# Compressed interaction network on one core: a smaller copy of layer 0's weights, another order of the first loads, and layer 2's weights read during the first two periods

## The chip, the cores and the metric

The kernel runs on one core of one Trainium2 chip. The metric is device time in microseconds (us) of one execution, as the median of several; lower is better. Engines are named as in the profile: PE multiplies matrices, DVE works element by element, ACT evaluates functions and copies, POOL does a little setup, and SP issues the transfers, which sixteen DMA engines carry out.

## The reference

For 512 rows of 39 fields of 32 numbers, three layers each form all products of a field with a hidden row, multiply them by a weight matrix and apply a ReLU:

```python
hidden = x                                        # [512, 39, 32]
for i in range(3):
    z = jnp.einsum('bmd,bnd->bmnd', x, hidden).reshape(B, -1, D)
    cur = jax.nn.relu(jnp.einsum('bcd,co->bod', z, Ws[i]) + bs[i][None, :, None])   # 200 rows out
    if i != 2: hidden, direct = cur[:, :100], cur[:, 100:]
    else:      direct = cur
    finals.append(direct)
return jnp.sum(jnp.concatenate(finals, axis=1), axis=-1)                            # [512, 400]
```

W0 is [39 x 39, 200]; W1 and W2 are [39 x 100, 200]; all is float32.

## The kernel before

The 512 x 32 pairs of row and position are cut into 128 units of 128 columns. For a unit, DVE forms products (L361 for layer 0, L380 for layers 1 and 2, L367 for four chunks of layer 2 that are multiplied whole), ACT rounds them to a high part (L525), DVE subtracts to get a low part (L384), and PE multiplies both by the weights, which are held in a high and a low part side by side in the `w_split` tiles (L659, L660; L647 for the whole chunks). Products live in a ring of three buffers. PE transposes the hidden half (L671), ACT spreads it (L541 to L544), and so the next layer's products can be made.

The order of the work is written out by hand, for each engine apart, and semaphores tie the engines together. In the steady state a period n handles layer 1 of unit n, layer 0 of unit n + 2 and layer 2 of unit n - 1. Period 0, ahead of the function `period`, has layer 1 of unit 0 and layer 0 of unit 2 alone; period 1 is the first with layer 2. A loop runs four periods at a time.

Ahead of period 0 stands the prologue, which the change rewrites:

- Layer 0 needs each unordered pair of fields once, so it needs the sum of two reads of W0: one along columns, one along rows, both starting at the diagonal and wrapping around after field 38. To let a plain strided read wrap, SP first copies W0 in DRAM to two tensors that hold it one and a half to two times over: `w0_columns_again` (L227, L228) and `w0_rows_again` (L229, L230). After both copies have landed, six loads (L241, L244) bring the strided rows into `pair_w` and `pair_w2`, 39 SBUF rows for each of three shifts; a seventh (L247) brings the bias. DVE adds the two (L413), ACT and DVE split the sum (L553, L416). The two buffers lie inside tile `xb0`.
- x is turned in DRAM into `x_by_unit`, one batch of units at a time (`turn_x`, L185 and L186), from where `load_pairs` (L191, L192) and `load_xb` (L198 to L204) fetch each unit's operands.
- W1 and W2 come in four groups each (`load_w`, L213, L215, L221, L223) through two staging halves inside tile `xb1`, numbered k = 0 to 7. For each group ACT writes the high part (L553), DVE the low part (L349). The last group of a layer has seven extra loads of four rows each (L221), after DVE has zeroed their rows (L345).
- PE's first multiplication of layer 1 waits until all eight groups are split, W2's too (L687).

SP issues every transfer, in one queue; an issue that waits for a semaphore holds all that stand behind it.

Of the kernel before, what the change touches and what calls it, by code (L numbers as in the profile page):

```python
# [5 lines left out]
F32 = mybir.dt.float32  # L6
# [4 lines left out]
P = 128  # L11
# [17 lines left out]
XROWS = F + SHIFTS * L0_CHUNKS - 1  # L29

# [47 lines left out]
def cin_kernel(nc, r_x, W0, W1, W2, b0, b1, b2, out):  # L78
    x, w0 = r_x.tensor, W0.tensor
    xt = nc.dram_tensor("x_by_unit", [UNITS, XROWS, T], F32)  # L80
    w0c = nc.dram_tensor("w0_columns_again", [F, 2 * F, O], F32)
    w0r = nc.dram_tensor("w0_rows_again", [2 * F, F, O], F32)
    xt_t, w0c_t, w0r_t = xt.ap().tensor, w0c.ap().tensor, w0r.ap().tensor

    with ExitStack() as ctx:
# [19 lines left out]
        z = [sb(f"z{i}", [P, GROUP * T]) for i in range(RING)]  # L105
# [10 lines left out]
        o_row = {l: sb(f"o_row{l}", [BT, DIRECT[l]]) for l in range(3)}  # L116
# [42 lines left out]
        stage_all = xb[1][:, :, :].rearrange("p c t -> p (c t)")  # L159

        def stage(k):
            at, n = (k % 2) * GROUP * O, group_chunks(k % GROUPS)
            return stage_all[:, at:at + n * O].rearrange("p (c o) -> p c o", o=O)
# [5 lines left out]
        pair_w = xb[0][:, :, :].rearrange("p c t -> p (c t)")[:, 0:L0_CHUNKS * O].rearrange("p (c o) -> p c o", o=O)  # L169
        Q = L0_CHUNKS * O  # L170
        pair_w2 = xb[0][:, :, :].rearrange("p c t -> p (c t)")[:, Q:2 * Q].rearrange("p (c o) -> p c o", o=O)

# [5 lines left out]
        def _(sp):  # L178
# [29 lines left out]
            def load_w(k, w, bias):  # L208
                g = k % GROUPS
                a, n = GROUP * g, group_chunks(g)  # L210
                wt, row = w.tensor, HID * O
                st = stage(k)
                sp.dma_start(st[0:MAIN, :, :], bass.AP(wt, a * row, [[O, MAIN], [row, n], [1, O]])).then_inc(w_in[k], 16)  # L213
                if g < GROUPS - 1:
                    sp.dma_start(st[MAIN:P, :, :],  # L215
                                 bass.AP(wt, CHUNKS * row + 32 * g * O, [[O, P - MAIN], [row, n], [1, O]])).then_inc(w_in[k], 16)
                else:
                    for j in range(TAIL_M):
                        n = min(TAIL_CHUNKS, F - TAIL_CHUNKS * j)
                        at = MAIN + TAIL * j  # L220
                        sp.dma_start(st[at:at + TAIL, 0:n, :],  # L221
                                     bass.AP(wt, TAIL_CHUNKS * j * row + MAIN * O, [[O, TAIL], [row, n], [1, O]])).then_inc(w_in[k], 16)
                    sp.dma_start(st[ONES_ROW:ONES_ROW + 1, 0, :], bass.AP(bias.tensor, 0, [[O, 1], [1, O]])).then_inc(w_in[k], 16)  # L223

            turn_x(0, 0)
            n2 = XROWS - F
            sp.dma_start(bass.AP(w0c_t, 0, [[2 * F * O, F], [1, F * O]]), bass.AP(w0, 0, [[F * O, F], [1, F * O]])).then_inc(w0_again[0], 16)  # L227
            sp.dma_start(bass.AP(w0c_t, F * O, [[2 * F * O, F], [1, n2 * O]]), bass.AP(w0, 0, [[F * O, F], [1, n2 * O]])).then_inc(w0_again[0], 16)  # L228
            sp.dma_start(bass.AP(w0r_t, 0, [[F * O, F], [1, F * O]]), bass.AP(w0, 0, [[F * O, F], [1, F * O]])).then_inc(w0_again[1], 16)  # L229
            sp.dma_start(bass.AP(w0r_t, F * F * O, [[F * O, n2], [1, F * O]]), bass.AP(w0, 0, [[F * O, n2], [1, F * O]])).then_inc(w0_again[1], 16)  # L230
# [3 lines left out]
            turn_x(0, 1)  # L234
            sp.wait_ge(cleared, 2)
            sp.wait_ge(w0_again[0], 32)
            sp.wait_ge(w0_again[1], 32)
            for k in range(SHIFTS):
                last = len(range(k, L0_PAIRS, SHIFTS))
                at = slice(k * F, (k + 1) * F)  # L240
                sp.dma_start(pair_w[at, 0:last, :],  # L241
                             bass.AP(w0c_t, k * O, [[(2 * F + 1) * O, F], [SHIFTS * O, last], [1, O]])).then_inc(pairs_w_in, 16)
                c = 1 if k == 0 else 0
                sp.dma_start(pair_w2[at, c:last, :],  # L244
                             bass.AP(w0r_t, (k + SHIFTS * c) * F * O, [[(F + 1) * O, F], [SHIFTS * F * O, last - c], [1, O]]))\
                  .then_inc(pairs_w_in, 16)
            sp.dma_start(pair_w[L0_ONES:L0_ROWS, 0, :], bass.AP(b0.tensor, 0, [[O, 1], [1, O]])).then_inc(pairs_w_in, 16)  # L247
            load_w(0, W1, b1)
            load_w(1, W1, b1)
# [4 lines left out]
            for k in range(2, 2 * GROUPS):  # L254
                sp.wait_ge(w_low_done, k)
                if k % GROUPS == GROUPS - 1:
                    sp.wait_ge(stage_ready, k // GROUPS + 1)
                load_w(k, W1 if k < GROUPS else W2, b1 if k < GROUPS else b2)
                if k == GROUPS - 1:
                    sp.wait_ge(ones_set, 1)  # L260
                    for g in range(GROUPS):
                        load_xb(0, 0, g)
            sp.wait_ge(xt_done, 96)
            turn_x(0, 3)
            sp.wait_ge(xt_done, 128)
            turn_x(1, 0)
            sp.wait_ge(product, 2)
            load_pairs(2)
            sp.wait_ge(ones_set, 2)
            for g in range(GROUPS):  # L270
                sp.wait_ge(xb_in[g], XB_COUNT[g])
                load_xb(1, 1, g)

            def send(l, rows):
                sp.wait_ge(o_in[l], rows + 1)
                sp.dma_start(bass.AP(out.tensor, rows * (BT * OUT_COLS) + OUT_AT[l], [[OUT_COLS, BT], [1, DIRECT[l]]]), o_row[l][:, :])\
                  .then_inc(o_out[l], 16)
# [65 lines left out]
        def _(dve):  # L343
            def stage_zeros(k):
                return nc.vector.memset(stage(k)[MAIN:P, :, :], 0.0)  # L345

            def low_w(k, dst, st):
                dve.wait_ge(w_high_done, k + 1)
                nc.vector.tensor_tensor(dst[:, :, O:2 * O], st, dst[:, :, 0:O].bitcast(F32), ALU.subtract).then_inc(w_low_done, 1)  # L349
# [6 lines left out]
            def product0(u, number, slot):  # L356
                slot_read(number)
                dve.wait_ge(pairs_in, 96 * (u + 1))
                left = x_left[0:L0_ROWS, :].unsqueeze(1).to_broadcast([L0_ROWS, L0_CHUNKS, T])
                dst = z[slot][0:L0_ROWS, 0:L0_CHUNKS * T].rearrange("p (c t) -> p c t", t=T)  # L360
                nc.vector.tensor_tensor(dst, left, x_right[0:L0_ROWS, :, :], ALU.mult).then_inc(product, 1)  # L361
# [7 lines left out]
            def product12(layer, u, par, g, number, slot):  # L369
# [9 lines left out]
                dst = z[slot][:, 0:n * T].rearrange("p (c t) -> p c t", t=T)  # L379
                nc.vector.tensor_tensor(dst, left, xb[par][:, c0:c0 + n, :], ALU.mult).then_inc(product, 1)  # L380

            def lows(number, slot, rows, n):
                dve.wait_ge(high, number + 1)
                nc.vector.tensor_tensor(z_low[slot][0:rows, 0:n * T], z[slot][0:rows, 0:n * T],  # L384
# [9 lines left out]
            def directs(l, rows, q):  # L394
# [8 lines left out]
                else:  # L403
                    dve.wait_ge(direct_in[l], u)
                    nc.vector.scalar_tensor_tensor(direct[l][:, :], part, 0.0, direct[l][:, :], ALU.max, ALU.add).then_inc(direct_in[l], 1)  # L405

            nc.vector.memset(x_left[MAIN:P, :], 1.0).then_inc(ones_l0, 1)
            nc.vector.memset(x_right[MAIN:P, :, :], 1.0).then_inc(ones_l0, 1)
            nc.vector.memset(pair_w, 0.0).then_inc(cleared, 1)
            nc.vector.memset(pair_w2, 0.0).then_inc(cleared, 1)  # L410
# [4 lines left out]
            dve.wait_ge(w_high_done, 1)  # L415
            nc.vector.tensor_tensor(w_split[0][0:L0_ROWS, :, O:2 * O], pair_w[0:L0_ROWS, :, :],  # L416
                                    w_split[0][0:L0_ROWS, :, 0:O].bitcast(F32), ALU.subtract).then_inc(w_low_done, 1)
            product0(0, 0, 0)
            lows(0, 0, L0_ROWS, L0_CHUNKS)
            for k in range(2 * GROUPS):  # L420
                l, g = 1 + k // GROUPS, k % GROUPS
                low_w(1 + k, piece(l, g), stage(k)[:, split_from(l, g):, :])
                if k in (1, 5):
                    dve.wait_ge(w_low_done, k + 2)
                    stage_zeros(k + 2).then_inc(stage_ready, 1)
                if k == 1:
                    dve.wait_ge(w_low_done, 1)
                    nc.vector.memset(xb[0][MAIN:P, TAIL_AT:CHUNKS, :], 1.0).then_inc(ones_set, 1)
                    product0(1, 1, 1)
                    lows(1, 1, L0_ROWS, L0_CHUNKS)  # L430
                    sums(0, 0)
                if k == 2:
                    directs(0, 0, 0)
                if k == 3:
                    sums(0, 1)
            dve.wait_ge(w_low_done, 1 + 2 * GROUPS)
            nc.vector.memset(xb[1][MAIN:P, TAIL_AT:CHUNKS, :], 1.0).then_inc(ones_set, 1)


            directs(0, 0, 1)  # L440
# [7 lines left out]
            lows(at + 4, slot_of(at + 4), L0_ROWS, L0_CHUNKS)  # L448
            sums(1, 0)
            sums(0, 2)  # L450
            directs(1, 0, 0)
            directs(0, 0, 2)

            def period(m, j, base, sl, layer0=True, before0=True, before2=True, last_low=True):
# [5 lines left out]

                product12(1, n, par, 0, base, slot(0))
                if last_low:
                    lows(base - 1, slot(-1), P, group_chunks(3))
# [57 lines left out]
        def _(act):  # L521
# [36 lines left out]
            for k in range(2 * GROUPS):  # L558
# [13 lines left out]
                if k == 5:  # L572
                    dup(0, 1)
# [198 lines left out]
```

## Time and profile before

| | |
|---|---|
| median of 3 runs | 2790.6 us (2790.5 to 2791.17) |
| the profiled execution's own time | 2791.72 us |
| its span, first to last instruction | 2790.0 us |
| PE busy | 2702.3 us, 97% |
| DVE busy | 2667.3 us, 96% |
| ACT busy | 1698.4 us, 61% |
| DMA, mean | 120 GB/s |

The span is what lies between the first and the last instruction; the execution has 1.7 us around it. In the profile's forty slices (69.75 us each) PE is over 90% busy in all but the first two: the prologue lies in these. A busy PE need not be at its peak, so what a wait costs is read from when the next stage starts.

### The profile page before, as it was taken

To read this page: it belongs to the slowest core of one execution; us is meant where nothing else is said; L and a number is where in the kernel's file an instruction comes from. 1 tells how busy PE (TensorE), PEld (TensorE's weight loads), DVE (VectorE), ACT (ScalarE), POOL (GpSimd) and SP (SyncE) were. 2 spreads that over 40 slices of the span, in tenths; PEclk is the share of its full clock that TensorE was granted. 3 is DMA by queue.
4 is the path that set the end of the run, shared out by engine and by line. 5 is a ranking of instruction groups with operands and counts; after the bars stand their busy time and mean duration, and the time that the engine had idled before them with its cause. 6 is when DMAs were issued, how large, how long until landed. Compare 5 with 4: busy or idle time off the path is not lost.

```text
span 2790.0 us, 56206 instructions
## 1 busy us (share of the span) xinstructions
PE 2702.3 (97%) x18112; PEld 2661.2 (95%) x18112; DVE 2667.3 (96%) x3218; ACT 1698.4 (61%) x3179; POOL 1.2 (0%) x11
## 2 busy tenths in 40 slices
PE   1799999999999999999999999999999999999999
PEld 1799999999999999999999999999999999999998
DVE  3799999999999999999999999999999999999997
ACT  2566666666666666666666666666666666666664
POOL 0000000000000000000000000000000000000000
PEclk9999999999999999999999999999999999999999
DMA  8454544454554454454454454445444445444541
GB/s 194 109 128 110 129 122 108 120 133 108 125 128 109 114 139 109 115 131 115 108 136 117 109 128 124 108 125 128 108 121 122 118 116 132 112 111 123 127 108 59
DMA packets 346786, 333.97 MB, mean 120 GB/s; under 512 B 151970, under 2 KB 281614, under 8 KB 346638
## 3 DMA queue, kind: packets, MB, share of 16 engines
q1 hardware_dynamic: 346762, 333.67, 48.0%
q8 instruction: 13, 0.21, 0.0%
q14 instruction: 11, 0.09, 0.0%
HBM read 332.73 MB, written 8.37 MB: 122 GB/s over the span
## 4 chain that ended last, share of the span: by engine, by line
PE 82%; DVE 8%; issue 4%; DMA 3%; ACT 2%; SPq 1%; DVEq 0%; ACTq 0%
PE acc L659 51%; PE acc L660 24%; PE acc L647 5%; DVE z_low L384 4%; DVE z L380 2%; DMA xb<-x_by_unit 1%; PE summed L677 1%; PE turned L671 1%; ACT z_high L525 1%; DMA xb<-in_L_rec_b_dram 1%; DVE z L361 1%; ACT hid L544 0%; DMA w_rows_again<-in_L_rec_W_dram 0%; DMA xb<-in_L_rec_W_dram 0%; DVE w_split L349 0%
## 5 line engine op out<-in xcount | busy, mean ns | idle before, releaser
L659 PE MATMUL acc<-w_split,z_high 128*128 128x400 f32 (+1 forms) x8320 | 2511.8, 369 | 64.6 <-DVE z_low L384 58.5
L660 PE MATMUL acc<-w_split,z_low 128*128 128x200 f32 (+1 forms) x8320 | 2120.5, 255 | 0.0
L525 ACT ACTIVATE z_high<-z 128x1024 fp32r<-128x1024 f32 (+3 forms) x1152 | 1125.0, 977 | 882.4 <-DVE z L380 728.3
L659 PEld LDWEIGHTS acc<-w_split,z_high 128*128 128x128 f32 (+1 forms) x8320 | 1565.4, 188 | 88.5 <-issue 78.4
L660 PEld LDWEIGHTS acc<-w_split,z_low 128*128 128x128 f32 (+1 forms) x8320 | 1593.0, 191 | 0.0
L384 DVE TENSOR_TENSOR z_low<-z,z_high 128x1024 fp32r<-128x1024 f32 (+3 forms) x1152 | 1282.5, 1113 | 45.3 <-ACT z_high L525 45.0
L380 DVE TENSOR_TENSOR z<-hid,xb 128x1024 f32<-128x1024 f32 (+2 forms) x1024 | 1142.0, 1115 | 11.2 <-DMA xb<-x_by_unit 10.9
L544 ACT ACTIVATE hid<-turned 32x128 f32<-32x128 f32 x768 | 205.3, 267 | 8.9
L541 ACT ACTIVATE hid<-turned 96x512 f32<-96x512 f32 x256 | 150.4, 588 | 91.8 <-PE turned L671 91.6
L647 PE MATMUL acc<-w_whole,z_whole 128*128 128x200 f32 x1024 | 197.7, 336 | 3.1 <-DVE s L391 3.1
L647 PEld LDWEIGHTS acc<-w_whole,z_whole 128*128 128x128 f32 x1024 | 168.9, 190 | 3.4 <-DVE s L391 3.4
L391 DVE TENSOR_TENSOR s<-acc,half 128x200 f32<-128x200 f32 x384 | 137.1, 357 | 8.9 <-ACT half L530 8.9
L361 DVE TENSOR_TENSOR z<-x_left,x_right 118x896 f32<-118x896 f32 x128 | 138.4, 1081 | 0.0
L530 ACT ACTIVATE half<-acc 128x200 f32<-128x200 f32 x384 | 126.9, 331 | 16.4 <-PE acc L660 10.9
L367 DVE TENSOR_TENSOR z_whole<-hid,xb 128x512 f32<-128x512 f32 x128 | 87.5, 684 | 5.8 <-ACT hid L544 5.8
L671 PE MATMUL turned<-ident,s 128*128 128x128 f32 x256 | 69.9, 273 | 16.5 <-ACT s L535 16.5
L405 DVE SCALAR_TENSOR_TENSOR direct<-s,direct 128x100 f32<-128x100 f32 (+1 forms) x288 | 83.0, 288 | 0.1
L542 ACT ACTIVATE hid<-turned 32x128 f32<-32x128 f32 x256 | 69.3, 271 | 3.0
L535 ACT ACTIVATE s<-s 128x24 f32<-128x24 f32 x256 | 52.4, 205 | 1.3 <-DVE s L391 1.3
L671 PEld LDWEIGHTS turned<-ident,s 128*128 128x128 f32 x256 | 36.0, 141 | 17.1 <-ACT s L535 17.1
L550 ACT ACTIVATE o_row<-summed 16x100 f32<-16x100 f32 (+1 forms) x96 | 25.5, 266 | 37.2 <-PE summed L677 36.4
L677 PE MATMUL summed<-direct,group_b 128*16 128x100 f32 (+1 forms) x192 | 38.5, 282 | 1.2 <-DVE direct L405 1.2
(25 smaller groups left out, 72.0 us busy)
## 6 DMA issues: line engine op xcount, KB each, us to landing
xb<-x_by_unit SPq DMA_DIRECT2D x384, 384.0 KB, 4.4
x_right<-x_by_unit SPq DMA_DIRECT2D x384, 136.5 KB
xb<-x_by_unit SPq DMA_DIRECT2D x384, 128.0 KB, 5.0
xb<-x_by_unit SPq DMA_DIRECT2D x128, 336.0 KB
xb<-x_by_unit SPq DMA_DIRECT2D x128, 84.0 KB
x_left<-x_by_unit SPq DMA_DIRECT2D x384, 19.5 KB
xb<-in_L_rec_W_dram SPq DMA_DIRECT2D x6, 600.0 KB, 9.4
x_by_unit<-in_r_x_dram SPq DMA_DIRECT2D x128, 19.5 KB
```

The lines of the kernel that those rows point to most:

```text
L361: nc.vector.tensor_tensor(dst, left, x_right[0:L0_ROWS, :, :], ALU.mult).then_inc(product, 1)
L380: nc.vector.tensor_tensor(dst, left, xb[par][:, c0:c0 + n, :], ALU.mult).then_inc(product, 1)
L384: nc.vector.tensor_tensor(z_low[slot][0:rows, 0:n * T], z[slot][0:rows, 0:n * T], z_high[slot][0:rows, 0:n * T].bitcast(F32), ALU.subtract ...
L391: nc.vector.tensor_tensor(s[l][:, :, 0:HID], acc[l][:, 0:O].rearrange("p (h o) -> p h o", o=HID), half[l][:, :, :], ALU.add)\
L525: nc.scalar.activation(z_high[slot][0:rows, 0:n * T], z[slot][0:rows, 0:n * T], ACT.Copy).then_inc(high, 1)
L530: nc.scalar.activation(half[l][:, :, :], acc[l][:, O:2 * O].rearrange("p (h o) -> p h o", o=HID), ACT.Copy)\
L541: nc.scalar.activation(h[0:MAIN, :, :], turned[l][0:MAIN, 0:T].unsqueeze(1).to_broadcast([MAIN, GROUPS, T]), ACT.Relu)
L544: last = nc.scalar.activation(h[MAIN:P, g, :], turned[l][32 * g:32 * (g + 1), 0:T], ACT.Relu)
L647: last = nc.tensor.matmul(acc[2][:, 0:O], z_whole[par][:, c * T:(c + 1) * T], w_whole[:, c, :], start=(c == 0), stop=False, skip_group_che ...
L659: nc.tensor.matmul(a[:, 0:2 * O], z_high[slot][0:rows, tok], w, start=(c == 0), stop=False, skip_group_check=True)
L660: last = nc.tensor.matmul(a[:, 0:O], z_low[slot][0:rows, tok], w[:, 0:O], start=False, stop=(c == chunks - 1), skip_group_check=True)
L671: nc.tensor.transpose(turned[l][:, 0:T], s[l][:, 0, :], ident[:, :]).then_inc(turned_in[l], 1)
```

## The change

Four things move.

1. The copies in DRAM hold only what must wrap. `NEAR` is 20, `REST` is 19. For fields 0 to 19 the six strided loads read W0 itself. For fields 20 to 38 they read two small copies, written by four copies of 19 rows of 3800 numbers. So layer 0's weights come in twelve loads and a bias instead of six and a bias, and DVE waits for 13 where it waited for 7.
2. Buffers: `pair_w` and `pair_w2` lie in the ring of products, now one tile `z`; groups 0 and 1 of W1, and all groups of W2, are staged in a tile `stage2` of their own, and only groups 2 and 3 of W1 in `xb1`. The rows for the outputs lie in `stage2` too.
3. SP's order: W0's first parts, the pairs of unit 0, W0's rest, then W1's groups, each followed by the part of `xb` that period 0 multiplies with it, then W2's first two groups, and W2's last two behind the `xb` of unit 1.
4. W2's groups are split on ACT and DVE in period 0 (the first) and period 1 (the other three), and PE waits for W1 alone ahead of period 0, for W2 ahead of period 1's layer 2. The layer-1 sums of unit 0 and layer-0 sums of unit 2 move from the gap between the two periods into period 1.

The core of the diff (the waits and the reordering of ACT and PE are of the same kind as DVE's):

```diff
+NEAR = L0_PAIRS
+REST = F - NEAR
...
-    w0c = nc.dram_tensor("w0_columns_again", [F, 2 * F, O], F32)
-    w0r = nc.dram_tensor("w0_rows_again", [2 * F, F, O], F32)
+    w0c = nc.dram_tensor("w0_columns_again", [REST, 2 * REST, O], F32)
+    w0r = nc.dram_tensor("w0_rows_again", [2 * REST, REST, O], F32)
...
+            def load_w0(near):
+                f0, n = (0, NEAR) if near else (NEAR, REST)
+                cols, rows = (w0, w0) if near else (w0c_t, w0r_t)
+                per_col, per_row = (F, F) if near else (2 * REST, REST)
+                for k in range(SHIFTS):
+                    last = len(range(k, L0_PAIRS, SHIFTS))
+                    at = slice(k * F + f0, k * F + f0 + n)
+                    sp.dma_start(pair_w[at, 0:last, :],
+                                 bass.AP(cols, k * O, [[(per_col + 1) * O, n], [SHIFTS * O, last], [1, O]])).then_inc(pairs_w_in, 16)
...
-            sp.dma_start(bass.AP(w0c_t, 0, [[2 * F * O, F], [1, F * O]]), bass.AP(w0, 0, [[F * O, F], [1, F * O]])).then_inc(w0_again[0], 16)
...
+            for half, (col, row) in enumerate([(NEAR, NEAR), (0, 0)]):
+                sp.dma_start(bass.AP(w0c_t, half * REST * O, [[2 * REST * O, REST], [1, REST * O]]),
+                             bass.AP(w0, w0_rest + col * O, [[F * O, REST], [1, REST * O]])).then_inc(w0_again[0], 16)
+                sp.dma_start(bass.AP(w0r_t, half * REST * REST * O, [[REST * O, REST], [1, REST * O]]),
+                             bass.AP(w0, row * F * O + NEAR * O, [[F * O, REST], [1, REST * O]])).then_inc(w0_again[1], 16)
+            sp.wait_ge(cleared, 2)
+            load_w0(True)
+            sp.dma_start(pair_w[L0_ONES:L0_ROWS, 0, :], bass.AP(b0.tensor, 0, [[O, 1], [1, O]])).then_inc(pairs_w_in, 16)
             sp.wait_ge(xt_done, 32)
             sp.wait_ge(ones_l0, 2)
             load_pairs(0)
-            turn_x(0, 1)
...
+            load_w0(False)
+            turn_x(0, 1)
+            sp.wait_ge(ones_set, 1)
+            for g in range(2):
+                load_w(sp, 1, g, W1, b1)
+                load_xb(0, 0, g)
...
-            dve.wait_ge(pairs_w_in, 16 * 7)
+            dve.wait_ge(pairs_w_in, 16 * 13)
...
-            pe.wait_ge(w_low_done, 1 + 2 * GROUPS)
-            pe.wait_ge(w_whole_in, 1)
+            pe.wait_ge(w_low_done, 1 + GROUPS)
...
+                else:
+                    pe.wait_ge(w_low_done, 1 + 2 * GROUPS)
+                    pe.wait_ge(w_whole_in, 1)
                 multiply_whole(n - 1, 1 - j % 2)
```

What stands on SP's queue near its start, before the change: the four copies and then the first loads of unit 0's pairs. The last column is rows by columns of the destination.

```order
L227 DMA w_columns_again<-in_L_rec_W_dram 39x7800
L228 DMA w_columns_again<-in_L_rec_W_dram 39x4000
L229 DMA w_rows_again<-in_L_rec_W_dram 30x10140
L230 DMA w_rows_again<-in_L_rec_W_dram 16x9750
L191 DMA x_left<-x_by_unit 39x128
L192 DMA x_right<-x_by_unit 39x7x128
```

The same place of the changed program: four copies of 19 rows, then the first of six loads that read W0 itself.

```order
L247 DMA w_columns_again<-in_L_rec_W_dram 19x3800
L249 DMA w_rows_again<-in_L_rec_W_dram 19x3800
L247 DMA w_columns_again<-in_L_rec_W_dram 19x3800
L249 DMA w_rows_again<-in_L_rec_W_dram 19x3800
L237 DMA z<-in_L_rec_W_dram 20x7x200
L240 DMA z<-in_L_rec_W_dram 20x6x200
```

Each copy has 19 rows of 15.2 KB where the first one had 39 of 31.2 KB. Further down SP's queue in the changed program, behind the pairs of unit 0, stand the six loads from the copies, then the second batch of x and W1's first group.

```order
L214 DMA x_right<-x_by_unit 39x7x128
L237 DMA z<-w_columns_again 19x7x200
L240 DMA z<-w_rows_again 19x6x200
L237 DMA z<-w_columns_again 19x7x200
L240 DMA z<-w_rows_again 19x7x200
L237 DMA z<-w_columns_again 19x6x200
L240 DMA z<-w_rows_again 19x6x200
L207 DMA x_by_unit<-in_r_x_dram 624x1x8
L208 DMA x_by_unit<-in_r_x_dram 320x1x8
L182 DMA stage<-in_L_rec_W_dram 96x8x200
```

These six loads had 39 rows each before; all W1 loads stand behind them. On DVE, in period 1, the changed program has this between its second and its third product of layer 1:

```order
L403 TENSOR_TENSOR z<-hid_1,xb 128x1024
L407 TENSOR_TENSOR z_low<-z,z_high 128x1024
L414 TENSOR_TENSOR s<-acc,half 128x2x100
L425 TENSOR_SCALAR direct<-s 128x100
L363 TENSOR_TENSOR w_split<-stage,w_split 128x8x200
L369 MEMSET stage 32x1400
L403 TENSOR_TENSOR z<-hid_1,xb 128x1024
L407 TENSOR_TENSOR z_low<-z,z_high 128x1024
L428 SCALAR_TENSOR_TENSOR direct<-s,direct 128x100
L363 TENSOR_TENSOR w_split<-stage,w_split 128x8x200
L403 TENSOR_TENSOR z<-hid_1,xb 128x896
```

Before, the products and low parts of that place followed each other directly; now sums, two low parts of W2 (L363) and a memset stand among them.

## Rows read from the trace of the kernel before

**Rows 1.** Chain that ended last, first 140 us: start, length in us, what.

```profile
5.26 11.92 DMA w_rows_again<-in_L_rec_W_dram
20.25 7.89 DMA xb<-in_L_rec_b_dram
...
76.06 1.38 ACT w_split L553
77.46 1.62 DVE w_split L349
...
115.54 1.37 PE acc L647 x8
```

**Rows 2.** Timeline: start, us, engine, line, operation, count, idle before and its releaser.

```profile
28.16 1.62 DVE L413 TENSOR_TENSOR xb<-xb 118x1400 f32<-118x1400 f32 x1 [23.11 <-DMA xb<-in_L_rec_b_dram]
62.05 0.87 ACT L562 ACTIVATE w_whole<-xb 128x800 f32<-128x800 f32 x1 [8.70 <-DMA xb<-in_L_rec_W_dram]
80.34 2.35 DVE L380 TENSOR_TENSOR z<-hid,xb 128x1024 f32<-128x1024 f32 x2
```

**Rows 3.** PE's waits from 140 us to 2780 us: total, times, longest.

```profile
PE acc L647 <- DVE s L391: 3.1, 1, 3.1
```

**Rows 4.** Windows, 157 to 240 us: busy us of PE, PEld, DVE, ACT, POOL.

```profile
157.00:240.00 83.00, 83.00 (x561) 81.84 (x561) 81.58 (x100) 51.69 (x99) 0.00 (x0) 1.00 0.48 117
```

**Rows 5.** DMA packets that start from 4.0 to 5.4 us, in 40 slices.

```profile
GB/s 21 13 14 3 0 0 0 0 0 891 3566 1783 891 1783 1783 891 0 0 0 0 0 0 0 0 0 0 0 0 0 0 0 0 0 0 0 0 0 0 0 0
DMA packets 75, 0.41 MB, mean 291 GB/s; under 512 B 62, under 2 KB 62, under 8 KB 62
```

**Rows 6.** Windows; the last two columns are DMA share of sixteen engines and GB/s.

```profile
6.00:10.00 4.00, 0.00 (x0) 0.00 (x0) 0.00 (x0) 0.00 (x0) 0.00 (x0) 1.00 0.86 314
7.00:7.50 0.50, 0.00 (x0) 0.00 (x0) 0.00 (x0) 0.00 (x0) 0.00 (x0) 1.00 1.50 624
...
20.00:22.00 2.00, 0.00 (x0) 0.00 (x0) 0.00 (x0) 0.00 (x0) 0.00 (x0) 1.00 0.90 147
42.00:60.00 18.00, 4.36 (x15) 3.99 (x15) 6.81 (x8) 6.09 (x11) 0.00 (x0) 1.00 1.06 223
72.00:72.50 0.50, 0.00 (x0) 0.00 (x0) 0.19 (x1) 0.28 (x1) 0.00 (x0) 1.00 1.14 381
73.50:74.50 1.00, 0.00 (x0) 0.00 (x0) 0.64 (x1) 0.00 (x0) 0.00 (x0) 1.00 0.27 69
```

**Rows 7.** SP's issues in the timeline: start, us taken to issue.

```profile
8.83 4.86 SPq L185 DMA_DIRECT2D x_by_unit<-in_r_x_dram  x1
...
70.04 2.50 SPq L221 DMA_DIRECT2D xb<-in_L_rec_W_dram  x7
```

**Rows 8.** DMA issues of the whole run: KB each, median us to landing.

```profile
out_dram<-o_row SPq DMA_DIRECT2D x64, 6.2 KB, 1.4
```

**Rows 9.** Window of PE's first eight chunks of layer 1, columns as in rows 4.

```profile
84.00:88.50 4.50, 4.39 (x16) 4.39 (x17) 4.50 (x5) 1.06 (x1) 0.00 (x0) 1.00 0.86 240
```

**Rows 10.** Timeline: the splitting of W2, the hidden rows of layer 0, two sums.

```profile
63.71 0.99 DVE L349 TENSOR_TENSOR w_split<-xb,w_split 128x800 fp32r<-128x800 f32 x1 [9.96 <-ACT w_split L553]
64.64 1.54 ACT L553 ACTIVATE w_split<-xb 128x1600 fp32r<-128x1600 f32 x1 [0.96 <-DMA xb<-in_L_rec_W_dram]
...
66.21 1.82 DVE L349 TENSOR_TENSOR w_split<-xb,w_split 128x1600 fp32r<-128x1600 f32 x1 [1.51 <-ACT w_split L553]
...
68.39 1.23 DVE L345 MEMSET xb<- 32x1400 f32 x1 [0.35 <-DVE w_split L349]
...
77.34 0.57 ACT L541 ACTIVATE hid<-turned 96x512 f32<-96x512 f32 x1
...
78.21 0.82 ACT L544 ACTIVATE hid<-turned 32x128 f32<-32x128 f32 x3
...
96.09 0.37 DVE L391 TENSOR_TENSOR s<-acc,half 128x200 f32<-128x200 f32 x1 [2.70 <-ACT half L530]
98.14 0.37 DVE L391 TENSOR_TENSOR s<-acc,half 128x200 f32<-128x200 f32 x1 [1.69 <-ACT half L530]
```

More of the change, by code:

```diff
@@ L206, in load_xb @@
                       .then_inc(xb_in[g], 16)
[L208 to L223, printed above, removed]
@@ L253, in _ @@
             load_pairs(1)
[L254 to L262, printed above, removed]
+            for g in range(2, GROUPS):
+                load_w(sp, 1, g, W1, b1)
+                load_xb(0, 0, g)
             sp.wait_ge(xt_done, 96)
             turn_x(0, 3)
+            for g in range(2):
+                sp.wait_ge(w_low_done, g + 2)
+                load_w(sp, 2, g, W2, b2)
+            sp.wait_ge(product, 2)
+            load_pairs(2)
             sp.wait_ge(xt_done, 128)
             turn_x(1, 0)
-            sp.wait_ge(product, 2)
-            load_pairs(2)
+            sp.wait_ge(w_low_done, 5)
             sp.wait_ge(ones_set, 2)
@@ L418, in _ @@
+            dve.wait_ge(w_low_done, 1)
             product0(0, 0, 0)
             lows(0, 0, L0_ROWS, L0_CHUNKS)
[L420 to L435, printed above, removed]
@@ L436, in _ @@
-            dve.wait_ge(w_low_done, 1 + 2 * GROUPS)
-            nc.vector.memset(xb[1][MAIN:P, TAIL_AT:CHUNKS, :], 1.0).then_inc(ones_set, 1)
+            low_piece(1, 1, 0)
+            sums(0, 0)
+            low_piece(2, 1, 1)
+            product0(1, 1, 1)
+            lows(1, 1, L0_ROWS, L0_CHUNKS)
+            directs(0, 0, 0)
+            low_piece(3, 1, 2)
+            sums(0, 1)
+            low_piece(4, 1, 3)
+            dve.wait_ge(w_low_done, 5)
+            ones(1)
             directs(0, 0, 1)
@@ L447, in _, with period @@
             lows(at + 3, slot_of(at + 3), P, group_chunks(3))
[L448 to L454, printed above, removed]
+            low_piece(5, 2, 0)
+            def period(m, j, base, sl, layer0=True, before0=True, before2=True):
                 n, par = m * QUARTERS + j, j % 2
@@ L459, in slot @@
                     return (sl + p) % RING
+                second = not before2
                 product12(1, n, par, 0, base, slot(0))
-                if last_low:
+                if second:
+                    lows(base - 1, slot(-1), L0_ROWS, L0_CHUNKS)
+                    sums(1, 0)
+                else:
                     lows(base - 1, slot(-1), P, group_chunks(3))
-                if before0 and last_low:
-                    directs(0, m + (j + 1) // QUARTERS, (j + 1) % QUARTERS)
+                    if before0:
+                        directs(0, m + (j + 1) // QUARTERS, (j + 1) % QUARTERS)
                 product12(1, n, par, 1, base + 1, slot(1))
                 lows(base, slot(0), P, group_chunks(0))
+                if second:
+                    sums(0, 2)
+                    directs(1, 0, 0)
+                    low_piece(6, 2, 1)
+                    dve.wait_ge(w_low_done, 7)
+                    stage_zeros(2)
                 product12(1, n, par, 2, base + 2, slot(2))
                 lows(base + 1, slot(1), P, group_chunks(1))
+                if second:
+                    directs(0, 0, 2)
+                    low_piece(7, 2, 2)
                 product12(1, n, par, 3, base + 3, slot(3))
@@ L495, in period @@
                     sums(0, n + 2)
-            period(0, 1, first(1), first(1) % RING, before2=False, last_low=False)
+            period(0, 1, first(1), first(1) % RING, before2=False)
             period(0, 2, first(2), first(2) % RING)
@@ L524, in highs @@
                 act.wait_ge(product, number + 1)
-                nc.scalar.activation(z_high[slot][0:rows, 0:n * T], z[slot][0:rows, 0:n * T], ACT.Copy).then_inc(high, 1)
+                nc.scalar.activation(z_high[slot][0:rows, 0:n * T], z[0:rows, slot, 0:n * T], ACT.Copy).then_inc(high, 1)
             def second_half(l, u, last):
@@ L590, in slot @@
                     return (sl + p) % RING
+                second = not before2
                 highs(base, slot(0), P, group_chunks(0))
-                if before0:
+                if second:
+                    second_half(1, 0, base - 2)
+                elif before0:
                     dup(0, n + 1)
                 highs(base + 1, slot(1), P, group_chunks(1))
-                hidden(1, n - 1, 1 - par)
+                if second:
+                    second_half(0, 2, base - 1)
+                    dup(1, 0)
+                    high_piece(2, 1)
+                    dup(0, 2)
+                else:
+                    hidden(1, n - 1, 1 - par)
                 highs(base + 2, slot(2), P, group_chunks(2))
+                if second:
+                    hidden(1, 0, 0)
+                    high_piece(2, 2)
                 if before2:
@@ L608, in period @@
                     q = 5
+                if second:
+                    high_piece(2, 3)
                 if j == 2:
@@ L702, in period @@
                 acc_free(1, n)
+                second = not before2
                 multiply(1, base, slot(0), 0)
-                if before0:
+                if before0 and not second:
                     transpose(0, n + 1)
@@ L708, in period @@
                 multiply(1, base + 1, slot(1), 1)
+                if second:
+                    transpose(1, 0)
+                    transpose(0, 2)
                 if j == 2:
```

145 lines of the change are left out of this document (78 added, 67 removed).

## The prediction

> **What bounds the kernel now.** I read the chain of waits of the first 140 us, then the timeline of that stretch, then the waits of the rest. From about 140 us on PE is the pace: it waits 3.1 us for one operation and little else up to 2780 us [rows 3]; between 157 and 240 us PE is busy 83.00 of 83 us and DVE 81.58 [rows 4], so DVE has only some 1.4 us of room in four periods. The prologue is another matter. PE's first multiplication of whole chunks, the mark where layer 2 of unit 0 begins, is at 115.54 us [rows 1]; from there the two programs do the same work, some 2674 us of it. So the change is worth what it moves this mark.
>
> I cut the time up to the mark in three. First, W0: DVE can add the two reads of W0 at 28.16 us, after waiting 23.11 us for a DMA [rows 2]; behind it stand the copy (11.92 us at 5.26) and the loads (7.89 us at 20.25) [rows 1]. Second, from there to the first product of layer 1 at 80.34 us [rows 2], 52.2 us, in which W1 and W2 arrive through two halves of one buffer; ACT alone waits 8.70 us for W2's first group [rows 2]. Third, from that product to the mark, 35.2 us.
>
> **Part 1, W0: how many DMA engines a transfer of 19 rows uses.** The first copy has 39 rows of 31.2 KB. Of the packets that start between 4.0 and 5.4 us 75 - 62 = 13 are over 8 KB, 0.41 MB or 13 x 31.2 KB; they start within 0.3 us, and then none starts for 0.8 us, though 26 rows of this copy, and more copies, are queued [rows 5]. So 13 engines work, three rows each, not sixteen. Near 74 us the seven loads of four rows of W2's last group drain: DMA share 0.27, which is 4.3 of sixteen engines, at 69 GB/s [rows 6]; they were issued within 2.5 us [rows 7], so had each taken other engines, all sixteen would have been at work. What fits both rows: the rows are dealt in equal shares, 13 x 3 and 4 x 1, always to the same first engines. A transfer of 19 rows then has equal shares only on one engine, since no number from 2 to 16 divides 19; one of 20 rows has ten.
>
> The Trainium skill ("DMA: Bandwidth & Descriptors", section "Why a DMA increments its semaphore by 16 and not by 1") states this as a rule: the transfer runs on the largest k up to 16 that divides the slowest dimension of both sides, and on this queue on the lowest-numbered k engines. By that rule the changed copies and the loads from them have k = 1; the trace agrees at 39 and 4 rows, and no run here shows 19. The Trainium skill's same page (section "Specifications") gives about 27 GiB/s per engine, by which the four copies would take an estimated 40 us.
>
> The terms, then:
> - Copies: 4 x 19 x 15,200 B = 1.155 MB through one engine. A busy engine moves GB/s over 16 x share: 624/(16 x 1.50) = 26.0 GB/s at best and 314/(16 x 0.86) = 22.8 over four us of the copies [rows 6]. I take 26.0, as nothing else disturbs one engine: 44.4 us (at 22.8: 50.7). From 4.0 us: 48.4. Before, the four copies (3.6 MB) took from 4 to 17.2 us [rows 1], three times the bytes in a third of the time.
> - Behind them on the same engine lie its shares of the loads from W0 itself (78 rows of 800 B) and of unit 0's pairs (72 rows of 512 B), 99 KB at 16 GB/s: 6.2 us. They cover SP's wait for the copies.
> - The six loads from the copies: 19 x 39 = 741 rows of 800 B, 0.593 MB. For rows of this size an engine moved 69/(16 x 0.27) = 16.0 GB/s where four worked, 381/(16 x 1.14) = 20.9 at best, 147/(16 x 0.90) = 10.2 where 13 read these same layouts [rows 6]. I take 16.0, the row with the fewest engines: 37.1 us (28.4 to 58.1).
> - Landing: 1.4 us, as for a small output [rows 8].
>
> W0 is complete at 48.4 + 6.2 + 37.1 + 1.4 = 93.1 us instead of 28.2: **+64.9 us**. Nothing hides it: W1's loads stand behind on the same queue, and everything on DVE, ACT and PE starts from W0. The loads behind may run ahead on the fifteen idle engines, but SP was held 4.86 us in one issue when about 130 rows per engine lay queued [rows 7], and one engine's share of all that follows is still to come; I take nothing for it, and up to 6 us as its bound.
>
> **Part 2, from W0 to the first product of layer 1.** W2 no longer stands here. What must land is W1 (3066 KiB), three parts of `xb` (1536), the pairs of unit 1 (468) and two batches of x (60): 5.25 MB, at the 223 GB/s of the long full stretch [rows 6] 23.6 us, plus 1.4 to land [rows 8]. Then the last group is split, a memset and one sum follow: 76.06 to 80.34 before, 4.3 us [rows 1, 2]. Together 29.3 instead of 52.2: **-22.9 us**. The work on ACT and DVE in between (each W1 group about 1.5 and 1.8 us) is shorter than the loads and hidden by them. Bounds: 24 us if loads run ahead, 35 if the 223 GB/s is too high by a fifth.
>
> **Part 3, the first product to the mark.** W2's split now lies here. DVE has four low parts, 0.99 + 1.82 + 1.82 + 1.62, and the memset, 1.23: 7.5 us [rows 1, 10], on an engine without room. Each low part waits for ACT's high part, and ACT's own queue decides: for the first group twice 0.87 us, whole and split half [rows 2]; for the second 1.54, less a short sum; for the last about 1.4 after ACT's products. The third is worst: ACT does it after the hidden rows of unit 0, these wait for PE's transposes, those for eight chunks on PE (4.39 us at half clock [rows 9], near half that at full), and these eight wait for a low part that DVE now makes only after the second group and its memset. From that low part: 2.2 to 4.4 for PE, two transposes, 1.7 for the hidden rows (0.57, then four short ones, three of which take 0.82) and 1.54 for ACT's high part [rows 10], 6 to 8 us in which DVE has nothing else. I add 1.9 + 1.3 + 7 + 1.9 = 12 us of waits. Taken away: DVE's 2.70 and 1.69 us ahead of the sums between the periods [rows 10], since a product now comes first. 35.2 + 7.5 + 12 - 4.4 = 50.3: **+15.1 us**. Bounds: 43 (waits covered) to 55.
>
> W2's loads of 0.8 MB each land far ahead of this, except the last, issued when the second group is split: 2.50 us for its small issues [rows 7] and 3 us of data at 223 GB/s, within the third group's wait.
>
> **Sum.** 64.9 - 22.9 + 15.1 = +57.1 us at the mark. After it DVE leads PE by about 2 us less; with its 1.4 us of room per four periods that could show as up to 2 us more, which I leave in the range. On the profiled execution's 2791.7 us (span 2790.0 and 1.7 around it) this is 2848.8; the median of the runs is 1.1 lower, so **2847 us**.
>
> **Rivals.**
> - *Rows dealt over many engines.* If 19 rows went to 16 engines unevenly, the change does what its parts promise: copies 1.155 MB at 314 GB/s [rows 6], 3.7 us; SP issues nineteen more transfers up to about 15 us, and W0 lands near 20. Then 20 + 29.3 + 50.3 = 99.6, 15.9 before the old mark: 2775 us, faster. It decides the sign, from the point where copies and loads together take under about 30 us. Against it: 39 rows went to 13, where an uneven deal would have used 16.
> - *One engine per transfer, but another each time.* Copies side by side, 289 KB at 26 GB/s, 11.1 us; each load 133 rows, 6.7 us; W0 near 25 us: 2780. Against it: the seven loads of four rows stayed on 4.3 engines.
> - *One engine, and the loads at 10.2 GB/s*, the rate at which these layouts were read: 58.1 instead of 37.1 us, 2868. For it: the same strides; against it: then 13 engines and the turning of x shared the memory.
>
> **How the numbers follow.** The forecast has 0.80; its own range is 2829 (loads at 20.9 GB/s and 6 us of running ahead, 8.7 + 6 less, and part 3 at its low end) to 2864 (copies at 22.8, +6.3, part 2 and 3 at their high ends). The slow loads have 0.10, the many engines 0.06, other engines 0.03; 0.01 is left for a mixture near no change. A difference of 0.2%, 5.6 us, is what a measurement of this kernel can tell from none. Slower by more: 0.90; faster: 0.09; same: 0.01. The range takes in the slow loads: 2829 to 2868.
>
> **What would show it.** In the trace after: between about 5 and 45 us packets over 8 KB start one at a time, near 0.6 us apart, with a DMA share near 0.06 of sixteen; SP stands in the issues of the loads; DVE waits for W0 until some 93 us (81 to 115); the first product of layer 1 comes about 29 us later, the mark about 50 after that; in period 1 DVE waits 6 to 8 us for ACT ahead of W2's third group, and PE starves with it. Four or more large packets starting together in the copies, or W0 complete ahead of 35 us, would prove the first step wrong, and the sign with it.

## The result, and the profile after

The changed kernel takes 2834.9 us (median of four runs, 2833.5 to 2835.5) where the kernel before takes 2790.65: a ratio of 1.0158, with a 95% interval of 1.014 to 1.0175. It is slower by 44.3 us; forecast was 2847, slower by 56.

The profiled execution took 2835.5 us. Part 1 of its page, the span and the busy time of the engines:

```profile
span 2833.8 us, 56212 instructions
PE 2705.9 (95%) x18112; PEld 2664.7 (94%) x18112; DVE 2668.2 (94%) x3218; ACT 1696.6 (60%) x3179; POOL 1.2 (0%) x11
```

The engines work as long as before (PE 2702.3, DVE 2667.3); the span alone is longer. So the time is a wait, and the chain that ended last shows where. First its longest pieces ahead of 100 us, then the mark that the prediction uses, the first multiplication of whole chunks:

```profile
5.28 4.75 SPq L237
10.08 8.38 SPq L240
18.50 4.49 SPq L237
23.04 8.51 SPq L240
31.59 8.49 SPq L237
40.12 5.80 SPq L240
...
50.23 3.97 SPq L240
54.24 3.90 SPq L237
58.19 4.66 SPq L240
62.88 4.70 SPq L237
67.63 3.90 SPq L240
71.57 4.13 SPq L207
...
97.25 8.52 DMA xb<-in_L_rec_b_dram
...
160.40 1.37 PE acc L688 x8
```

Where the copies and the loads stood in the chain of before [rows 1], SP now stands in the very issues of the loads of W0 (L237, L240), up to 8.5 us in one. The mark is at 160.40 instead of 115.54, 44.9 us later, and the span is 43.8 longer: from the mark on nothing was lost, 1.1 us was won (no run here was made to show why). DVE's timeline gives the two points between:

```profile
80.09 1.62 DVE L438 TENSOR_TENSOR z<-z 118x1400 f32<-118x1400 f32 x1 [72.64 <-DMA z<-w_rows_again]
...
110.08 2.35 DVE L403 TENSOR_TENSOR z<-hid,xb 128x1024 f32<-128x1024 f32 x2
```

W0 is complete at 80.09 where it was at 28.16 [rows 2]; its last transfer is one from the small copy `w_rows_again`. The windows of the stages, with DMA share and GB/s in the last two columns, say how it came:

```profile
25.00:30.00 5.00, 0.00 (x0) 0.00 (x0) 0.00 (x0) 0.00 (x0) 0.00 (x0) 1.00 0.06 27
55.00:75.00 20.00, 0.00 (x0) 0.00 (x0) 0.00 (x0) 0.00 (x0) 0.00 (x0) 1.00 0.07 23
80.00:106.00 26.00, 9.01 (x30) 7.84 (x30) 13.85 (x12) 10.53 (x16) 0.00 (x0) 0.81 1.04 226
```

One sixteenth is 0.0625: while the copies run, one engine moves 27 GB/s, and while the loads run, one engine moves 23. Before, all of this ran at 0.86 to 0.90 of sixteen engines [rows 6]. The packets of 4 us of the copies, in 40 slices, and their count:

```profile
GB/s 0 0 152 0 0 0 0 0 152 0 0 0 0 0 152 0 0 0 0 152 0 0 0 0 0 152 0 0 0 0 0 152 0 0 0 0 0 152 0 0
DMA packets 8, 0.11 MB, mean 27 GB/s; under 512 B 1, under 2 KB 1, under 8 KB 1
```

Seven rows of 15.2 KB start one behind the other, 0.5 to 0.6 us apart. In [rows 5] thirteen rows of 31.2 KB started at once.

### The profile page after: what moved, and what is told of

Its sections match the earlier page's. It is cut to its first block, busy times and chain, and to the rows that moved or that the text cites. A ratio compares the mean times of both kernels' runs of the same rounds, so it can differ in the third digit from the quotient of the medians.

```text
span 2833.8 us, 56212 instructions
## 1 busy us (share of the span) xinstructions
PE 2705.9 (95%) x18112; PEld 2664.7 (94%) x18112; DVE 2668.2 (94%) x3218; ACT 1696.6 (60%) x3179; POOL 1.2 (0%) x11
## 4 chain that ended last, share of the span: by engine, by line
PE 90%; SPq 4%; DVE 3%; issue 1%; ACT 1%; DMA 1%; DVEq 0%; ACTq 0%
PE acc L700 56%; PE acc L701 26%; PE acc L688 6%; SPq L240 1%; DVE z_low L407 1%; PE summed L718 1%; SPq L237 1%; PE turned L712 1%; DVE z L403 1%; DMA xb<-x_by_unit 1%; ACT z_high L553 0%; SPq L213 0%; DMA xb<-in_L_rec_b_dram 0%; ACT w_split L581 0%; ACT hid L572 0%
## 5 line engine op out<-in xcount | busy, mean ns | idle before, releaser
L438 DVE TENSOR_TENSOR z<-z 118x1400 f32<-118x1400 f32 x1 | 1.6, 1618 | 72.6 <-DMA z<-w_rows_again 72.6
L578 ACT ACTIVATE stage<-summed 16x100 f32<-16x100 f32 (+1 forms) x96 | 25.5, 266 | 37.4 <-PE summed L718 36.6
```

## The experiments

In the table, W0 is where DVE adds the two reads, the first product is that of layer 1, and the mark is the one above, each in the kernel's profiled execution. The kernel before was timed again beside each group: 2789.0 us for the first four, 2789.6 for the next four, 2787.8 for the last.

| kernel | W0 | first product | mark | median us | ratio to before, 95% |
|---|---|---|---|---|---|
| before | 28.2 | 80.3 | 115.5 | 2790.65 | |
| changed | 80.1 | 110.1 | 160.4 | 2834.9 | 1.0158 [1.014, 1.0175] |
| 16 and 3 rows | 24.1 | 53.1 | 102.7 | 2777.9 | 0.9956 [0.9939, 0.9972] |
| copies alone cut | 43.9 | 74.2 | 123.7 | 2797.6 | 1.0027 [1.0017, 1.0037] |
| loads alone cut | 59.5 | 90.2 | 138.8 | 2812.0 | 1.0087 [1.007, 1.0104] |
| W0 as before | 26.4 | 56.6 | 106.9 | 2780.8 | 0.9972 [0.9962, 0.9982] |
| 15 and 24 rows | 23.6 | 53.1 | 103.5 | 2778.1 | 0.9958 [0.9944, 0.9972] |
| smaller copy alone | 24.3 | 75.1 | 110.6 | 2785.2 | 0.9984 [0.9974, 0.9993] |
| ACT's order | 23.0 | 53.1 | 100.4 | 2775.2 | 0.9947 [0.9933, 0.996] |
| and DVE's order | 22.7 | 51.7 | 97.5 | 2772.5 | 0.9936 [0.9922, 0.9949] |
| and SP's order | 23.8 | 53.1 | 92.9 | 2768.1 | 0.9928 [0.9915, 0.9942] |

The mark of the kernel with the loads alone cut is taken from PE's timeline, 138.67, plus the 0.16 us by which the chain stands behind that view in the others. For the last three kernels, built one on the other, the intervals overlap from one to the next, so a single step of some 3 us is not clear by the time alone.

**Are the 19 rows the cause?** Every transfer of 19 rows of the changed kernel is cut into one of 16 and one of 3; nothing else differs.

```diff
+REST_ROWS = [(0, 16), (16, REST - 16)]
...
+                for r, m in REST_ROWS:
+                    sp.dma_start(bass.AP(w0c_t, half * REST * O + r * 2 * REST * O, [[2 * REST * O, m], [1, REST * O]]),
+                                 bass.AP(w0, w0_rest + col * O + r * F * O, [[F * O, m], [1, REST * O]])).then_inc(w0_again[0], 16)
...
+                    for r, m in [(0, n)] if near else REST_ROWS:
+                        at = slice(k * F + f0 + r, k * F + f0 + r + m)
```

> The changed kernel, with every transfer of 19 rows (four copies, six loads) cut into one of 16 and one of 3 rows; bytes, strides and order stay. Theory (19 rows run on one engine): copies about 5 us instead of 43, loads about 5 instead of 28, so W0 is complete near 20 us instead of 80, the mark (PE's first whole chunks) near 100 instead of 160, and the time about 2775 us, below the 2790.6 of before. Rival (the many small transfers, SP's order or the direct strided reads of W0 cost the time): ten more issues of 0.4 to 0.5 us make it no better than 2835 us, rather 2840.

It took 2777.9, some 57 us less than the changed kernel and 11.1 less than before. DVE's timeline:

```profile
24.11 1.62 DVE L442 TENSOR_TENSOR z<-z 118x1400 f32<-118x1400 f32 x1 [16.66 <-DMA z<-w_rows_again]
...
53.13 2.35 DVE L407 TENSOR_TENSOR z<-hid,xb 128x1024 f32<-128x1024 f32 x2
```

The same bytes through more transfers: W0 56 us earlier. The first rival of the prediction, in which the change does what its parts promise, had 2775 for this case.

**Copies and loads apart.** The same cut for the four copies alone, then for the six loads alone.

> Only the four copies are cut into 16 and 3 rows; the six loads keep 19. Theory: W0 gains the copies' 38 us but not the loads' 26: complete near 43 us, mark near 123, about 2798 us. Rival (the copies alone hold everything, the loads are as fast as before): near 2775 us, as with both cut.

> Only the six loads are cut into 16 and 3 rows; the copies keep 19. Theory: copies still end near 47 us, SP then issues twelve loads in some 5 us, W0 complete near 57 us, mark near 137, about 2812 us. Rival (the loads are hidden behind the copies anyway): no change from 2835 us.

Both came out within 1 us of what was expected. Cutting only the loads leaves the copies on one engine: W0 at 59.5, 35.4 us behind the kernel with both cut. Cutting only the copies leaves the loads there: 43.9, 19.8 us behind. Together 55.2, and the changed kernel is 56.0 behind: the two costs add up and explain all of it. SP's timeline of the kernel with the copies cut, at the loads (us taken to issue in the second column):

```profile
13.55 0.24 SPq L238 DMA_DIRECT2D z<-w_columns_again  x1
13.83 4.11 SPq L241 DMA_DIRECT2D z<-w_rows_again  x1
17.98 3.90 SPq L238 DMA_DIRECT2D z<-w_columns_again  x1
21.93 4.66 SPq L241 DMA_DIRECT2D z<-w_rows_again  x1
26.62 4.70 SPq L238 DMA_DIRECT2D z<-w_columns_again  x1
31.37 3.90 SPq L241 DMA_DIRECT2D z<-w_rows_again  x1
```

The issues of 4.66 and 4.70 us, and those of 3.90, are the same to 0.01 us as in the changed kernel 36 us later. Here SP issued only as fast as the one engine took rows off: the loads have 133 or 114 rows, and each of these issues lasts as long as the load ahead of it takes, so 4.70 / 133 is 35 ns for a row of 800 B, 23 GB/s.

**Is it the number of rows, or the number of transfers?** The first experiment also doubled the transfers. Here one number of the changed kernel is another, and nothing is cut:

```diff
-NEAR = L0_PAIRS
+NEAR = 15
```

> The changed kernel with one number changed: fields 0 to 14 are read from W0 itself and 24 fields from the copies, so the transfers have 15 and 24 rows; nothing is cut, and there are as many transfers as in the changed kernel. By equal shares of rows 24 rows go to 12 engines and 15 to 15. Theory: copies of 24 x 19.2 KB x 4 = 1.84 MB at 314 GB/s take 5.9 us, W0 is complete between 22 and 28 us, the mark is near 102: 2774 to 2779, with 57 us less than the changed kernel although more is copied. Rival (what cured it in the cut form was the number of transfers, or 19 rows were slow for their size or their place in DRAM and not for their number): W0 stays late, in proportion to bytes even later than 80 us, 2835 or more.

```profile
23.57 1.62 DVE L438 TENSOR_TENSOR z<-z 118x1400 f32<-118x1400 f32 x1 [16.11 <-DMA z<-w_rows_again]
```

2778.1 us: with 24 rows a transfer, as many transfers, and more bytes copied (1.84 instead of 1.16 MB), W0 is complete 56.5 us earlier than with 19. The rivals of count, size and place fall; how the rows divide over the engines is left. The packets of this kernel from 4.0 to 5.4 us, in 40 slices, show the division itself:

```profile
GB/s 9 11 1 0 0 0 0 0 0 1646 1097 549 1097 1097 0 0 0 0 0 0 0 549 0 0 549 0 0 0 0 0 0 0 0 0 0 0 0 0 0 0
DMA packets 38, 0.23 MB, mean 165 GB/s; under 512 B 26, under 2 KB 26, under 8 KB 26
```

Of the 24 rows of the first copy 38 - 26 = 12 start, and then none for half a microsecond, though more rows are queued: twelve engines.

**What the rest of the change is worth.** All of it, but W0's copies and loads as before.

```diff
-                f0, n = (0, NEAR) if near else (NEAR, REST)
-                cols, rows = (w0, w0) if near else (w0c_t, w0r_t)
-                per_col, per_row = (F, F) if near else (2 * REST, REST)
+                f0, n, cols, rows, per_col, per_row = 0, F, w0c_t, w0r_t, 2 * F, F
...
-            load_w0(True)
```

> The change without its first part: W0 copied and loaded as in the kernel before (39 rows), all the rest as changed. Theory: W0 complete near 28 us, then 30 us to the first product of layer 1 and 50 to the mark, as measured in the changed kernel: mark near 108, about 2784 us, 7 below before. Rival (the new order and the split of layer 2 do the harm, or give nothing): 2791 us or more.

```profile
26.43 1.62 DVE L434 TENSOR_TENSOR z<-z 118x1400 f32<-118x1400 f32 x1 [18.97 <-DMA z<-w_rows_again]
...
56.59 2.35 DVE L399 TENSOR_TENSOR z<-hid,xb 128x1024 f32<-128x1024 f32 x2
```

2780.8, some 3 us less than expected. From W0 to the first product 30.2 us instead of 52.2, from there to the mark 50.3 instead of 35.2: the order of the loads and the split of W2 gain 22.0 and cost 15.1, as the prediction had it (22.9 and 15.1).

**What the smaller copy is worth.** The kernel before with this part alone, its transfers cut as in the first experiment (the code is that of `load_w0` with `REST_ROWS`, ahead of the old order of loads).

> The kernel before with the smaller copy alone, its transfers of 19 rows cut into 16 and 3; every load of W1 and W2 and the order of ACT, DVE and PE are as before. With both parts of the change in this form W0 was complete at 24.1 us, before at 28.2, and with all but the smaller copy at 26.4 us. Theory: the copy is worth little by itself, since W0 comes some 4 us earlier, and what follows is paced by W1 and W2 arriving through two halves of one buffer: 2789.0 less 3 to 4, 2785 to 2786. Rival: the copy was what gave the 11 us of that kernel: about 2778. Second rival: the buffers' pace swallows even the 4 us: 2789.

2785.2, as expected. W0 comes 3.9 us earlier, and the mark 5.0; DVE's and then ACT's timeline show the old pace behind it:

```profile
24.28 1.62 DVE L427 TENSOR_TENSOR xb<-xb 118x1400 f32<-118x1400 f32 x1 [19.23 <-DMA xb<-w_rows_again]
...
75.09 2.35 DVE L394 TENSOR_TENSOR z<-hid,xb 128x1024 f32<-128x1024 f32 x2
```

```profile
57.38 0.87 ACT L576 ACTIVATE w_whole<-xb 128x800 f32<-128x800 f32 x1 [8.66 <-DMA xb<-in_L_rec_W_dram]
```

ACT still waits 8.66 us for W2's first group, as before [rows 2]. Alone the copy is worth 4.4 us and the order 8.2; together, in the first experiment, 11.1.

**The cost in period 1.** Of the 15.1 us, 9.2 are waits of DVE and 5.9 its work. The windows from the first product to the mark, before and in the changed kernel; DVE's busy time is the fourth number:

```profile
80.34:115.54 35.20, 27.00 (x155) 26.58 (x156) 28.21 (x31) 16.28 (x27) 0.00 (x0) 0.95 0.51 125
110.08:160.40 50.32, 30.64 (x155) 29.30 (x156) 34.12 (x35) 23.35 (x37) 0.00 (x0) 0.77 0.50 121
```

DVE's timeline in the changed kernel, at W2's four groups:

```profile
124.07 0.99 DVE L363 TENSOR_TENSOR w_split<-stage,w_split 128x800 fp32r<-128x800 f32 x1 [3.44 <-ACT w_split L581]
...
132.18 1.83 DVE L363 TENSOR_TENSOR w_split<-stage,w_split 128x1600 fp32r<-128x1600 f32 x1 [1.05 <-ACT w_split L581]
146.28 1.82 DVE L363 TENSOR_TENSOR w_split<-stage,w_split 128x1600 fp32r<-128x1600 f32 x1 [8.13 <-ACT w_split L581]
...
154.15 1.62 DVE L363 TENSOR_TENSOR w_split<-stage,w_split 128x1400 fp32r<-128x1400 f32 x1 [1.91 <-ACT w_split L581]
```

And ACT's, where the longest of them comes from:

```profile
142.98 0.59 ACT L569 ACTIVATE hid<-turned 96x512 f32<-96x512 f32 x1 [4.99 <-PE turned L712]
...
144.71 1.54 ACT L581 ACTIVATE w_split<-stage 128x1600 fp32r<-128x1600 f32 x1
```

ACT has nothing to do for 4.99 us but stands in the hidden rows of unit 0, and the high part that DVE waits for is queued behind them. Part of this wait is PE's clock. In the two windows, some eight chunks each, the granted clock is the third number from the end:

```profile
138.00:142.70 4.70, 4.67 (x17) 4.64 (x18) 0.15 (x1) 0.00 (x0) 0.00 (x0) 0.50 0.45 121
158.00:160.40 2.40, 2.28 (x15) 2.31 (x16) 2.40 (x3) 1.17 (x2) 0.00 (x0) 1.00 0.71 225
```

The chunks ahead of the transposes ran at 0.50 (1.2 GHz), after PE had stood idle from 133.1 to 138.0 us, and took 4.7 us; the last eight ahead of the mark, at 1.00 (2.4 GHz), took 2.3. So some 2.4 of the 8.13 us are the clock, an estimate from these two rows; no run changes the clock alone. Three kernels take such a place out of the way, each on top of the one before, starting from the 16 and 3 rows. First ACT:

```diff
                 if second:
+                    high_piece(2, 2)
                     hidden(1, 0, 0)
-                    high_piece(2, 2)
```

> The 16 and 3 form of the change, and in period 1 ACT makes the high part of W2's third group ahead of the hidden rows of unit 0 instead of behind them. In the changed kernel DVE waited 8.13 us there for ACT, which waited 4.99 us for PE's transposes. Theory: this wait was on the path to the mark, most of it goes, but the next wait (for the hidden rows or the last group) takes part of it back: about 3 us off the mark of 102.7 us, 2775. Rival: the hidden rows are what the products of layer 2 wait for next, and they now come 1.5 us later: the time stays at 2778 or grows to 2779.

```profile
82.38 1.83 DVE L367 TENSOR_TENSOR w_split<-stage,w_split 128x1600 fp32r<-128x1600 f32 x1 [1.30 <-ACT w_split L585]
...
86.95 1.09 DVE L388 TENSOR_TENSOR z<-x_left,x_right 118x896 f32<-118x896 f32 x1 [0.61 <-DMA x_right<-x_by_unit]
...
92.58 1.62 DVE L367 TENSOR_TENSOR w_split<-stage,w_split 128x1400 fp32r<-128x1400 f32 x1 [2.87 <-ACT w_split L585]
```

The wait went from 8.12 to 1.30 us, and the mark from 102.7 to 100.4: of 6.8 us a third was kept. Some 2.8 us went into DVE's other waits, and 1.6 into PE's clock at the last eight chunks ahead of the mark, here first in the kernel with 16 and 3 rows, then in this one:

```profile
100.40:102.60 2.20, 2.20 (x15) 2.20 (x16) 2.20 (x3) 1.10 (x2) 0.00 (x0) 1.00 0.82 242
96.50:100.30 3.80, 3.75 (x15) 3.75 (x16) 3.80 (x4) 1.39 (x2) 0.00 (x0) 0.55 0.83 254
```

Ahead of them PE stood idle for 0.3 us in the one and for 4.5 us in the other. Then DVE, with the low part of the second group and its memset behind a product's low part:

```diff
-                    low_piece(6, 2, 1)
-                    dve.wait_ge(w_low_done, 7)
-                    stage_zeros(2)
                 product12(1, n, par, 2, base + 2, slot(2))
                 lows(base + 1, slot(1), P, group_chunks(1))
                 if second:
+                    low_piece(6, 2, 1)
+                    dve.wait_ge(w_low_done, 7)
+                    stage_zeros(2)
                     directs(0, 0, 2)
```

> As the kernel with ACT's other order, and DVE's low part of W2's second group, with its memset (1.82 and 1.23 us), stands behind the low part of the second product of period 1 instead of ahead of it, so that PE's second group of chunks, and the transposes behind it, do not wait for them. Theory: 2 to 3 us more off the mark, 2772 to 2773. Rival: the last group of W2 is issued when the memset is done, so it lands later by the same 2 to 3 us and the mark stays: 2775.

```profile
77.82 1.82 DVE L367 TENSOR_TENSOR w_split<-stage,w_split 128x1600 fp32r<-128x1600 f32 x1
...
86.04 1.09 DVE L388 TENSOR_TENSOR z<-x_left,x_right 118x896 f32<-118x896 f32 x1 [4.26 <-DMA x_right<-x_by_unit]
```

2772.5, as expected, but of the 2.9 us off the mark 1.4 were there at the first product already (51.7 for 53.1), ahead of anything that the edit moves; 1.5 are the order's. The low parts of the second and third group now wait for nothing, and what ends last is a load that DVE waited only 0.61 us for in the kernel with ACT's order: the pairs of unit 3, which SP issues behind W2's last group. So SP:

```diff
+            sp.wait_ge(w_low_done, 6)
+            load_w(sp, 2, 2, W2, b2)
+            sp.wait_ge(xt_done, 160)
+            sp.wait_ge(product, first(0) + GROUPS + 1)
+            load_pairs(3)
+            sp.wait_ge(w_low_done, 7)
+            load_w(sp, 2, 3, W2, b2)
```

> As the kernel with both other orders, and SP issues the pairs of unit 3 ahead of W2's last group instead of behind it. In the kernel before it in this series the wait that was left in period 1 was DVE's, 4.26 us ahead of the product of layer 0, for x_right; SP issued these pairs from 80.36 us on, behind the seven small loads of W2's last group (2.33 us from 77.64), and it had been free from 66.9 to 76.1 us. Theory: this wait goes, and W2's last group, whose packets were through at about 84.5 us, is what ends next: 3 to 4 us off the mark of 97.4 us, 2769 us. Rival: the last group lands no earlier than ACT took it, 88.1 us: the mark stays, 2772.5.

```profile
82.61 1.08 DVE L389 TENSOR_TENSOR z<-x_left,x_right 118x896 f32<-118x896 f32 x1
...
86.61 1.62 DVE L368 TENSOR_TENSOR w_split<-stage,w_split 128x1400 fp32r<-128x1400 f32 x1 [1.91 <-ACT w_split L586]
```

The wait is gone, the mark is at 92.85, and the kernel takes 2768.1 us: 0.9928 of the kernel before, and the fastest of all. From the first product to the mark it takes 6.0 us less than with DVE's order: 4.2 for the wait, 1.8 because the last eight chunks ahead of the mark ran at a granted clock of 1.00 instead of 0.51. The three steps together are clear of noise: with all three the slowest run took 2768.8 us, with none the fastest 2775.0.

## Why the prediction was right, point by point

- **The deal of rows to engines** was the step on which the sign hung, and it held: share 0.06 to 0.07, one packet at a time, and the cure by 16 and 3 or by 15 and 24 rows. That the rows are dealt in equal shares, read from 39 rows and 4, was carried to 19 rightly. The rivals of many engines and of another engine each time are out. By the rule of the Trainium skill ("DMA: Bandwidth & Descriptors", section "Why a DMA increments its semaphore by 16 and not by 1") 19 rows have one engine, 24 rows twelve and 15 rows fifteen; the shares here show the one and the packets of the kernel with 24 rows the twelve; the fifteen is not shown by itself.
- **Copies:** 26.0 GB/s and through at 48.4 us were forecast; one engine moved 27, and its last packet over 8 KB started within 47.9 us and takes 0.6. Right.
- **Loads: the term that was mis-sized.** 741 rows at 16.0 GB/s, 37.1 us, were forecast; at the 35 ns a row of SP's issues it is 25.9. I had taken the row with the fewest engines at work; it was the tail of seven small loads, and even the best row, 20.9, was below what one engine does by itself. The 28.4 us that I kept as the lower end was not low enough.
- **Near loads and pairs on the same engine:** 6.2 us forecast. From W0 at 80.1, less copies to 48.4, loads 25.9 and landing 1.4, 4.4 are left. The 1.8 here and the 11.2 of the loads make the 13.0 us by which W0 was early (80.1 for 93.1), of which part 2, at 30.0 for 29.3, takes back 0.7: the mark came 12.2 us earlier than forecast, and the median is 12.1 lower.
- **Nothing hides it** held: DVE waited 72.6 us in one piece. I also had up to 6 us of loads running ahead on idle engines in the range; there was next to none, for SP stood in the issues of the six loads until 71.6 us, and W1's first load was issued at 77.4.
- **Part 2:** 29.3 forecast, 30.0 measured, at 226 GB/s where 223 was assumed.
- **Part 3:** 50.3 forecast and measured, but its terms were not all right. The waits ahead of the four low parts were 3.44, 1.05, 8.13 and 1.91, 14.5 us instead of 12. All of DVE's waits grew by 9.2 us where 12 less 4.4 were forecast, 1.6 too much, and its work by 5.9 instead of 7.5, 1.6 too little, mostly since it had less of the next work done at the mark. That the sum came out to 0.1 us is luck. The place and the cause of the largest, 6 to 8 us for the third group behind hidden rows, transposes and chunks, were as forecast, and the experiment with ACT's order shows that the wait came from ACT's queue. The "half clock" was misread: the clock column of [rows 9] says 1.00. Only the pace there, 0.55 us a chunk, is that of the stretch at 0.50 in the changed kernel, where PE took 4.7 us, a little beyond the 2.2 to 4.4 assumed.
- **After the mark** up to 2 us of loss was in the range; 1.1 were gained.
- **The sums:** 2848.8 less 1.1 is 2847.7, not 2847, and what is named for the lower end of the range, 8.7, 6 and 7.3 us less, leads to 2825, not 2829. The result lies inside either way.

## What to carry to other kernels

Before the rows of a transfer are cut down, see how the new number divides over the DMA engines: here half the rows took over three times as long (the copies 44 us for 13, with a third of the bytes), and a number with a large divisor up to sixteen (or a cut into 16 and the rest) cured it at no cost that shows (2778.1 and 2777.9 us). Price such a transfer from a row where one engine works alone, not from the tail of several. When a wait is taken out of a hand-written order, look at once for what is queued behind the next one: three moves of a few lines, each found in the trace of the last, took 9.8 us off the mark and some 8 off the time against the kernel before.

## What the runs showed of the hardware that I had not expected

One DMA engine alone moved rows of 800 B at 35 ns each, 23 GB/s, nearly the 27 GB/s that it reached with rows of 15.2 KB; with a mean of 14.4 of the sixteen at work on the same kind of rows each moved 10.2 [rows 6]. So small rows were slower here in company than by themselves; what they wait for then, no run here separates. And an issue on SP can take as long as the whole transfer before it, 4.70 us for 133 rows. It can also stand behind the copies: a load of 20 x 7 rows took 8.51 us to issue while the share was 0.06 and all but the one engine with the copies idle. So a transfer confined to one engine held back the queue for all sixteen; how much may lie queued before an issue is held, I did not measure.
